# Gated graph kernel: an opening on 64x64 squares with reordered queues, and the last state's subtraction on TensorE

## What is computed

```python
h = relu(layernorm(x))
q, k, v = h @ Wq.T, h @ Wk.T, h @ Wv.T
rel = adj.T * (q @ k.T)                       # 64x64 for each graph
rel = rel / norm(rel, axis=2)                 # each row by its length
x = x + rel @ v
h = h0 = relu(layernorm(x))
for _ in range(3):                            # gated graph unit
    a = adj @ h                               # in and out matrix are both adj
    av = concat(a, a)
    z = sigmoid(av @ w3.T + b3 + h @ u3.T + bu3)
    r = sigmoid(av @ w4.T + b4 + h @ u3.T + bu3)
    c = tanh(av @ w5.T + b5 + (r * h) @ u5.T + bu5)
    h = (1 - z) * h + z * c
out = x + h
```

## Time and profile before

| | |
|---|---|
| time, median of 3 runs | 883.26 us (882.33 to 884.26) |
| the profiled execution's own time | 878.96 us |
| its span, first to last instruction | 877.2 us |
| PE busy | 862.9 us, 98% |
| PEld busy | 706.7 us, 81% |
| DVE busy | 744.0 us, 85% |
| ACT busy | 492.7 us, 56% |
| POOL busy | 125.0 us, 14% |

### The profile page before, as it was taken

One profiled execution on the slowest core, in us unless ns is written; L12 is line 12 of the kernel. 1 busy time (PEld: TensorE's weight loads), 2 busy tenths in 40 slices (PEclk: granted clock), 3 DMA queues, 4 the chain that ended last, 5 costly groups with the idle time before them and its releaser, 6 DMA issues.

```text
span 877.2 us, 19374 instructions
## 1 busy us (share of the span) xinstructions
PE 862.9 (98%) x7356; PEld 706.7 (81%) x7356; DVE 744.0 (85%) x1518; ACT 492.7 (56%) x881; POOL 125.0 (14%) x161
## 2 busy tenths in 40 slices
PE   8999999999999999999999999999999999999997
PEld 7868888787887888878888888888888787788886
DVE  5988889888898888888989888888889888898666
ACT  5565655646456473665645656456555556555553
POOL 1110112201131020310103101120111301121000
PEclk9999999999999999999999999999999999999999
DMA  6014332533245233551424514155231543224222
GB/s 188 23 50 123 98 97 102 171 113 97 97 135 179 72 120 101 164 157 57 126 95 145 188 54 143 50 168 169 74 120 63 177 146 97 97 104 137 74 72 97
DMA packets 88451, 99.53 MB, mean 113 GB/s; under 512 B 8640, under 2 KB 80576, under 8 KB 88384
## 3 DMA queue, kind: packets, MB, share of 16 engines
q1 hardware_dynamic: 88384, 98.50, 35.4%
HBM read 50.76 MB, written 47.71 MB: 112 GB/s over the span
## 4 chain that ended last, share of the span: by engine, by line
PE 64%; DVE 13%; issue 9%; DMA 6%; ACT 4%; POOL 2%; SPq 2%; DVEq 0%; POOLq 0%; ACTq 0%
PE gate L438 9%; PE cand L433 7%; PE gate L433 7%; PE cand L435 7%; PE cand L434 7%; PE gate L434 6%; PE gate L435 6%; PE fea L590 4%; DVE c_s L1180 2%; DMA hx_trip<-hx 2%; DMA h_back<-h_trip 2%; PE fea L523 1%; PE tok L433 1%; DMA h_trip<-h_blk 1%; PE tok L434 1%
## 5 line engine op out<-in xcount | busy, mean ns | idle before, releaser
L860 ACT ACTIVATE r_s<-gate,b_r 128x512 f32<-128x512 f32 x96 | 60.7, 684 | 91.3 <-PE gate L438 91.1
L766 ACT ACTIVATE h_hi<-h 128x512 fp32r<-128x512 f32 x92 | 57.0, 630 | 65.8 <-DVE h L986 44.8
L766 ACT ACTIVATE rh_hi<-rh 128x512 fp32r<-128x512 f32 x96 | 58.9, 631 | 47.0 <-DVE rh L1212 47.0
L378 POOL TENSOR_TENSOR rstd<-vare,minus_half 128x4 f32<-128x4 f32 x32 | 42.2, 1318 | 292.2 <-DVE vare L1020 292.2
L433 PE MATMUL gate<-h_hi,W_hi_u 128*128 128x512 f32 x192 | 80.1, 417 | 0.2 <-DVE h_lo L986 0.2
L873 ACT ACTIVATE z_s<-gate,b_z 128x512 f32<-128x512 f32 x96 | 63.0, 680 | 29.4 <-PE gate L435 29.4
L433 PE MATMUL cand<-rh_hi,W_hi_u 128*128 128x512 f32 (+1 forms) x196 | 77.8, 397 | 1.2 <-DVE rh_lo L986 1.0
L1212 DVE TENSOR_TENSOR rh<-r_s,h 128x512 f32<-128x512 f32 x96 | 67.5, 743 | 12.2 <-ACT r_s L860 11.6
L435 PE MATMUL cand<-rh_hi,W_lo_u 128*128 128x512 f32 (+1 forms) x196 | 75.6, 385 | 0.0
L434 PE MATMUL cand<-rh_lo,W_hi_u 128*128 128x512 f32 (+1 forms) x196 | 75.5, 385 | 0.0
L433 PE MATMUL gate<-a_hi,W_hi_wz 128*128 128x512 f32 x192 | 74.8, 390 | 0.6 <-DVE W_lo_wz L986 0.6
(11 more groups left out here) (154 smaller groups left out, 2031.6 us busy)
## 6 DMA issues: line engine op xcount, KB each, us to landing
h_back<-h_trip SPq DMA_DIRECT2D x216, 128.0 KB, 2.8
h_trip<-h_turned SPq DMA_DIRECT2D x40, 512.0 KB, 2.6
x_s<-x SPq DMA_DIRECT2D x15, 512.0 KB, 5.1
out<-o_s SPq DMA_DIRECT2D x15, 512.0 KB, 3.5
hx_back<-hx_trip SPq DMA_DIRECT2D x56, 128.0 KB, 2.8
h_trip<-h_blk SPq DMA_DIRECT2D x14, 512.0 KB, 3.2
hx_trip<-hx SPq DMA_DIRECT2D x14, 256.0 KB, 3.2
hx_trip<-hx SPq DMA_DIRECT2D x28, 128.0 KB, 3.1
```

The source lines that it names most:

```text
L378: nc.gpsimd.tensor_tensor(rstd[n][:], vare[n][:], minus_half[:], ALU.pow).then_inc(rstd_ready[n], 1)
L766: return nc.scalar.activation(dst, src, ACT.Copy)
L860: nc.scalar.activation(r_s[:, c, :], gate[:, c, :], ACT.Sigmoid, bias=b_r[:, c:c + 1]).then_inc(r_ready, 1)
```

## The change

**Squares in the opening.** The opening uses `scores_by_set` and `weighted_sum` too. `v_hi`, `v_lo`, `S_hi`, `S_lo` and their splits are gone; DVE copies v (`take_v`) and masks by squares (`mask_by_set`). To have quarters 2 and 3 lie swapped, `transpose_hx` multiplies them with `ident_sw`, an identity with its halves swapped (two ACT copies), in place of a transpose.

**First statistics.** Tile 0's statistics, power and shift are done in halves. Of POOL's memsets those of adjT and mask go, one of minus_ident comes, and SP no longer waits for them ahead of the mask's loads. Tile 1's statistics are no longer cut in two around the splits.

**Queues.** PE: `product_m(0)` behind the first transposes; the norms of tile 0 (`norms_first`, into `gate`) behind the weighted sum; those of tile 1 (`norms_second`) behind `reset_gate_a`; `candidate_rh` of window 0 in two halves around `transpose_new(1, 1)`. ACT takes the copies to `h` from DVE, POOL the bias sums. POOL keeps tile 0's residual behind the second inverse deviation. DVE: `kept_part(0, 0)` ahead of tile 1's `h_lo`, the split of wz ahead of `add_attention`.

**The end.** PE computes ident*c_s - ident*d_s with `minus_ident` in true fp32, which gives the new state turned (`new_last`), in place of DVE's subtractions and the transposes; the output of tile 14 is added in two parts.

```diff
-    FEA_START = ["q 0", "rel 0", "norm 0", "q 1", "rel 1", "adj first", "norm 1", "adj 0"]
+    FEA_START = ["q 0", "rel 0", "q 1", "rel 1", "adj first", "norm 1", "adj 0"]
...
-            inverse_std(0, 0)
+            pool.wait_ge(vare_half, 1)
+            nc.gpsimd.tensor_tensor(rstd[0][:, 0:HQ], vare[0][:, 0:HQ], minus_half[:, 0:HQ], ALU.pow).then_inc(rstd_half, 1)
...
-            inverse_norm(fea_taken, 2 * n("norm 0") + 2)
+            inverse_norm(norm_taken, 1)
+            pool.wait_ge(bias_in, 16 * 5)
+            for dst, (m1, m2) in ((b_r, (2, 1)), (b_z, (0, 1)), (b_c, (3, 4))):
+                nc.gpsimd.tensor_tensor(dst[:], b_in[:, m1, :], b_in[:, m2, :], ALU.add).then_inc(bias_ready, 1)
             inverse_std(1, 0)
             inverse_norm(fea_taken, 2 * n("norm 1") + 2)
+            inverse_std(1, 1)
             keep_resid(0, 0)
-            inverse_std(1, 1)
             keep_resid(1, 1)
...
+                        if q < HQ:
+                            nc.tensor.transpose(out, src, ident[:])
+                        else:
+                            last = nc.tensor.matmul(out, src, ident_sw[:], start=True, stop=True)
...
+            def new_last(n):
+                pe.wait_ge(minus_ready, 1)
+                pe.wait_ge(diff_ready, 2 * LAST)
+                for e in range(2):
+                    tok_wait(n, e)
+                    pe.wait_ge(prod_ready, 2 * LAST + 2 * e)
+                    for q in range(HQ * e, HQ * e + HQ):
                         for c in range(C):
-                            last = nc.tensor.transpose(tok[:, q, c * P:(c + 1) * P], h[1][:, c, graph_pair(q)], ident[:])
+                            dst = tok[:, q, c * P:(c + 1) * P]
+                            one(dst, d_s[:, c, graph_pair(q)], minus_ident[:], start=True)
+                            last = one(dst, c_s[:, c, graph_pair(q)], ident[:], stop=True)
                     last.then_inc(tok_full, 1)
...
-            scores(n("rel 0"), n("q 0"))
+            scores_by_set(n("rel 0"), n("q 0"))
             values(0, n("v 0"), (1,))
             transpose_hx(1, cand, turned_full)
-            norms_start(0, n("norm 0"))
-            weighted_sum_start(0, n("sum 0"))
+            weighted_sum(n("v 0"), n("rel 0"))
+            norms_first()
...
             reset_gate_h_start()
-            norms_start(1, n("norm 1"))
-            weighted_sum_start(1, n("sum 1"))
+            weighted_sum(n("v 1"), n("rel 1"))
             pe.wait_ge(w_lo_ready, 5)
             reset_gate_a(0, 0, n("adj first"))
-            pe.wait_ge(h_new_ready, 2)
+            norms_second(n("norm 1"))
+            pe.wait_ge(h_copied, C)
             candidate_a(0, 0)
             update_gate(0, 0)
+            candidate_rh(0, 0, (0,))
             tok_done(n("sum 1"))
             transpose_new(1, 1, tokT, tok_full)
-            candidate_rh(0, 0)
+            candidate_rh(0, 0, (1,))
...
+            take_q(n("q 0"), (0,))
+            dve.wait_ge(x_in[1], 16)
+            stats_part(0, 1, range(Q))
+            take_q(n("q 0"), (1,))
             stats_end(0, 1)
...
-            copy_new_start(0, cand)
-            dve.wait_ge(bias_in, 16 * 5)
-            for dst, (m1, m2) in ((b_r, (2, 1)), (b_z, (0, 1)), (b_c, (3, 4))):
-                nc.vector.tensor_tensor(dst[:], b_in[:, m1, :], b_in[:, m2, :], ALU.add).then_inc(bias_ready, 1)
+            take_norm_second(n("norm 1"))
+            split_weight(6, "wz", sumz)
             add_attention(1, 1, n("sum 1"))
...
+            kept_part(0, 0)
             split_new_start(1, 1, tokT, tok_full, 2 * n("new 0"), tok_taken)
-            kept_part(0, 0)
-            copy_new_start(1, tokT)
+            dve.wait_ge(h_copied, 2 * C)
             update(1, 0, 1)
```

More of the change, by code:

```diff
@@ L503, in values @@
                     last.then_inc(tok_full, 1)
-            def scores(n, n_q):
-                pe.wait_ge(fea_taken, 2 * n_q + 2)
-                fea_wait(n, 0)
-                fea_wait(n, 1)
-                for q in range(Q):
-                    for c in range(C):
-                        last = nc.tensor.matmul(feaS[:, q, :], hxT[:, c, graph_pair(q)], q_s[:, c, graph_pair(q)],
-                                                start=c == 0, stop=c == C - 1)
-                last.then_inc(fea_full, 2)
             def scores_by_set(n, n_q):
@@ L653, in candidate_rh @@
                 pe.wait_ge(rh_lo_ready, 2 * w + 2)
-                for o in range(C):
+                for o in halves:
                     linear(cand[:, o, :], "u5", o, rh_hi, rh_lo, False, True).then_inc(c_full, 1)
@@ L776, in split_weight, with normalise_first @@
                 copy(W_hi[name][:].rearrange("p c n -> p (c n)"), src).then_inc(w_hi_ready, 1)
+            def normalise_first(quarters):
+                for q in quarters:
+                    nc.scalar.activation(hx[:, q, :], x_s[0][:, q, :], ACT.Relu, bias=shift[0][:, q:q + 1],
+                                         scale=rstd[0][:, q:q + 1]).then_inc(hx_ready, 1)
             def normalise(n, g, s, in_blocks=False):
@@ L849, in split_new_start, with copy_new_start @@
                     copy(h_hi[s][:, c, :], src[:, c, :]).then_inc(h_hi_ready, 1)
+            def copy_new_start(s, src, taken, count):
+                for c in range(C):
+                    act.wait_ge(taken, count + (c + 1))
+                    copy(h[s][:, c, :], src[:, c, :]).then_inc(h_copied, 1)
             def split_new(g, s):
@@ L971, in _ @@
             update_sigmoid(0)
+            copy_new_start(1, tokT, tok_taken, 2 * n("new 0"))
             candidate_tanh(0)
@@ L1163, in final @@
                 dve.wait_ge(h_in, 16 * BL * w)
-                for c in range(C):
+                for c in parts:
                     part = slice(c * P, (c + 1) * P)
@@ L1168, in final, with kept_part @@
                                                    resid[s][:, :, part].rearrange("p q (b f) -> p q b f", b=BL), ALU.add)
-                last.then_inc(final_ready, 1)
-            def kept_part(w, s):
-                for c in range(C):
+                if C - 1 in parts:
+                    last.then_inc(final_ready, 1)
+            def kept_part(w, s, parts=range(C)):
+                for c in parts:
                     dve.wait_ge(z_ready, 2 * w + (c + 1))
```

214 lines of the change are left out of this document (93 added, 121 removed).

## The result

The changed kernel takes 886.2 us (median of 10 runs, 884.61 to 888.05) against 883.12 us (median of 10 runs) before: ratio 1.004, 95% interval 1.0029 to 1.0052. It is slower, by 2.6 to 4.6 us. The profiled execution took 888.05 us with a span of 885.9, so it lies 1.9 us over its median, while that of before lies 4.2 us under the median of its ten runs. The two profiles are thus further apart (8.7 us of span) than the two kernels.

The account below looks back on a forecast made before the run. TensorE bounds 54.30 to 860 us, so only the opening, waits just behind it and the tail can move. 2.1 us to window 1, 0.9 behind, 0 tail: +3.0 on 883.26 gives 886.3 us, range 884.0 to 888.8.

Parts of the forecast that it names:

- first rival: Clock falls while PE idles about 4 us before window 0's candidate; costs 1.4 to 2.0 us, 887.9 us; chance 0.18.
- W0: First gate matmul of window 0: 1.3 us earlier, at 32.7 instead of 34.02 us.
- From W0 to r*h: Opening: norm products done at 40.0, DVE waiting about 3 us, reset_state at 46.5 against 46.11 us.
- The residual copy: POOL's copy for tile 0 beside DVE's rh and rh_lo operations: 0 to 0.37 us, taken as 0.37.
- From rh_lo to W1: From rh_lo's end at 49.6 to window 1's first gate matmul at 56.4: 6.8 us, against 5.5 now.
- Behind W1: After window 1's first gate matmul, ACT's h1 copies ahead of the tanh lengthen PE's wait for a_lo by 0.9 us.
- The tail: Program end: sixteen true fp32 matmuls subtract and turn, ending at 873.8 us again; change 0, bounds -0.3 to +0.5 us.

Follow-up runs that it names:

- the experiment on the residual copy: Changed kernel with GpSimd's two residual copies waiting until rh_lo of window 0 is done: 885.68 us, ratio 1.0025 to the kernel before.
- norms early: Changed kernel with tile 1's norm products back ahead of its weighted sum on TensorE: 882.82 us, ratio 0.9998 to the kernel before.
- all five moves: Changed kernel with norms, whole candidate and h_lo order undone, ScalarE's h copies behind the tanh, residual copies behind rh_lo: 878.03 us, ratio 0.9945.
- the squares alone: Kernel before with only the 64x64 squares for the opening's scores and weighted sums, v copied, S not split, queues unchanged: 880.98 us, ratio 0.9974.
- three moves undone: Changed kernel with norm products ahead of the weighted sum, candidate whole behind the transposes, h_lo ahead of d_s: 878.34 us, ratio 0.9952.
- h_lo first: Changed kernel with VectorE's split of tile 1's state ahead of the product d_s again: 885.58 us, ratio 1.0024 to the kernel before.
- tanh first: Changed kernel with ScalarE's copies of tile 1's state behind window 0's tanh, VectorE's wait behind its update: 886.21 us, ratio 1.0030.

## Why the prediction was right, and where it was not

The time was forecast at 886.3 us, between 884.0 and 888.8, and came out at 886.2. The sum that led there was not as good as that, and by the forecast's own signs (matmuls of twice the length near 50 us, a granted clock under 1 there) its first rival is what ran.

- **W0.** Forecast 1.3 us earlier, at 32.7. It was 33.66 and 33.23, but m, the arrival of Wq and Wk, was later there by 0.97 and 0.55 than in the profile I worked from. From m to W0 it is 24.98 and 24.97 us against 26.31 and 26.09: 1.1 to 1.3 earlier. The step was right, but it was counted from an execution in which the weights came early.
- **From W0 to r*h.** The norm products end 7.29 us behind W0, forecast 7.3. The attention add starts 9.63 behind it, forecast 9.4 (the power took 1.51 us beside the split of wz, not 1.38). r*h starts 13.98 behind, forecast 13.8. The DVE's wait was 3.09 us, forecast about 3.
- **The residual copy.** Taken at 0.37 us, with 0 to 0.37 as its bounds; it cost 0.79. The bound was too narrow: it came from a power on POOL, which reads four columns, and not from a copy of 1024. The forecast says that no row of before shows such a pair; the trace had one, at 39.68 us, with 0.86 us in it (the experiment on the residual copy). It also calls the power's 1.01 us its time alone, while the row at 38.57 lay beside DVE's copies out of the PSUM tile `cand` (38.52). What the forecast quotes of the Trainium skill ("Perfetto Trace Analysis", Optimizing Scalar/DVE Operations) on the port that VectorE and GpSimd share agrees with the trace in this: the later copy cost something, and more than I took. The traces show the slowdown, not the port.
- **From rh_lo to W1.** Forecast 6.8 us; it was 8.80. Without the fall of the clock it is 57.41 - 50.59 = 6.82. Each step of that chain was right.
- **The clock.** The forecast's rival, at 0.18, was what happened: PE stood idle for 4.69 us (forecast about 4; the residual and the power made most of the rest), and its price of 1.4 to 2.0 us was measured at 1.6 to 2.0. Against it I had set the 3.6 us behind 870.20, in which PE was busy for 1.34 and the clock stayed up. That stretch has no gap longer than 1.4 us, so it spoke for nothing here; the gap of 1.69 with the norms early left the clock up as well. Nor is the 1.00 that the forecast quotes for the warm-up a reading, since the trace of before has no record of the clock ahead of 5.48 us. With the clock the forecast named 887.9 us.
- **Behind W1.** Forecast 0.9 us; W1 to W2 grew by 0.8 (16.36 against 15.56) and c_s came 1.25 us behind W1, forecast 1.3.
- **The tail.** Forecast 0; 7.2 us in both, though 7.7 in the second profile of before.

The forecast has window 2 at +3.0 us. From m to W2 the two profiles of each kernel have 67.4 us on average against 62.0, so +5.4. The 2.4 us between them are the clock (1.6 to 2.0), the residual (0.4) and the power (0.1). The time moved by 3.1 us in the first comparison and 3.4 in the second, 1.9 to 5.0 with their intervals. So the middle of the forecast was met with an error of 2.4 us in the opening that the times don't show in full: as close as 0.1 us it was luck. The step that was short is the one from r*h to W1, with the clock put at nothing in the main sum. Why the times don't show it in full stays open. The other kernels have it too: their ratios are 0.6 to 2.4 us better than their m to W2 says (norms early +0.4 by the profile and -0.2 by the ratio; all five moves -3.1 and -4.9), in some of them within the interval, in the sum hardly by chance. The same kernel against itself came out 1.3 us on the other side. Taken off the medians, m to W2 leaves 818.8 to 820.4 us in the ten timings with the changed opening, 819.8 with the squares alone, and 820.3 to 822.8 in those of before. So 1 to 2 us seem to be gained outside that stretch by every kernel that has the squares, also the one without the new tail and the new queues. No run shows where; since the rounds differ by 4.6 us between two profiles of one kernel, it would take many more profiles to tell.

That the loss is real, and in the opening, does not hang on this: undoing the norms' place alone takes the ratio from 1.004 to 0.9998, and three moves undone take it to 0.9952.

## What to carry to other kernels

Ask of an instruction that is moved back in one queue what is waiting for it at the head of another in-order queue, and what stands behind that: here four small products, moved behind twelve matmuls, held up a vector queue for 3.1 us and with it a reset that TensorE needed. Price the idle stretch that such a wait gives TensorE twice, once for itself and once for the slower matmuls behind it, and find from profiles with shorter and longer gaps which ones are harmless. Look for the price of two engines at work side by side among all rows of the trace, small instructions too: a sum of two columns that took 1.01 us instead of 0.15 had it. Judge an edit of a microsecond by the distances between landmarks of the profile, which repeated here to 0.2 us (0.4 with the low clock between them), and only then by the total, which does not.

## What the runs showed of the hardware

- The granted clock fell in or just behind PE gaps of 4.68 and 4.69 us (changed kernel, h_lo first, tanh first) and of 3.90 us, and did not with a gap of 1.69. In the changed kernel's second profile it read 1.00 through the whole gap and fell behind the first matmul after it. What it cost differed with that: W0 to W1 took 26.25 and 25.87 us, where before it differed by 0.03.
- A copy of 128x1024 on POOL beside two 128x512 subtractions on DVE made these 2.08 us instead of 1.29; in the order with POOL late each took its own time (1.29 and 1.04). The same copy beside a sum of 128x2 on DVE made it 1.01 us, where the next such sum took 0.15. POOL's power of four columns took 1.01 us beside DVE copies out of PSUM, and 1.51 beside a weight split of DVE.
- The kernel before took 800.09 us from window 2 to the last candidate matmul in one execution and 804.70 in another, and the weights of the first product came at 7.71 and 8.64 us.
